# The start of a fused LoRA and expert kernel: fewer first loads, one tile's gather in two parts, another order

## The reference

```
g  = x Wg^T + 0.5 (x Ag[i]^T) Bg[i]^T          # i = itok_B_2_6[batch], rank 16
u  = x Wu^T + 0.5 (x Au[i]^T) Bu[i]^T
a  = silu(g) * u                               # 1376 columns
x += a Wd^T + 0.5 (a Ad[i]^T) Bd[i]^T          # layer 0
x += x W1[c]                                   # layer 1, c = itok_B_0_15[batch]
x += x W2^T + 2 * top-2 experts of 8 (LoRA)    # layer 2, bias by itok_B_0_7
x += x W3[c]                                   # layer 3
```

## Time and profile before

| what | value |
|---|---|
| median of three runs | 581.99 us (581.69 to 582.32) |
| the profiled execution | 581.79 us |
| its span | 579.5 us |
| PE busy | 569.5 us, 98% |
| DVE, ACT, POOL busy | 304.3, 206.5, 222.6 us |
| DMA | 77.38 MB, mean 134 GB/s |

### The profile page before, as it was taken

How to read it: one execution, slowest core, us unless ns; L and a number is a source line. 1 busy time by engine, 2 the same in 40 slices (tenths; PEclk the granted TensorE clock), 3 DMA queues, 4 the chain that set the end, 5 groups by cost and what they waited for, 6 DMA issues and landing times.

```text
span 579.5 us, 8822 instructions
## 1 busy us (share of the span) xinstructions
PE 569.5 (98%) x3381; PEld 513.9 (89%) x3381; DVE 304.3 (53%) x698; ACT 206.5 (36%) x413; POOL 222.6 (38%) x227
## 2 busy tenths in 40 slices
PE   7999999999999999999999999999999999999996
PEld 6888989898989898989898989898989899999995
DVE  5896353534343434444444444444444667777776
ACT  5774133333333333333232323233332533333331
POOL 4442153656565656441313131413130212443431
PEclk9999999999999999999999999999999999999999
DMA  8974343343534343442424242424242821243322
GB/s 268 379 248 143 110 144 95 122 153 123 154 122 154 122 153 128 147 155 77 138 77 137 77 139 76 137 78 137 77 138 73 300 84 54 74 136 139 111 90 74
DMA packets 35033, 77.38 MB, mean 134 GB/s; under 512 B 5360, under 2 KB 9776, under 8 KB 34992
## 3 DMA queue, kind: packets, MB, share of 16 engines
q0 software_dynamic: 10752, 37.23, 20.1%
q1 hardware_dynamic: 24096, 39.56, 20.1%
q10 hardware_dynamic: 144, 0.03, 0.0%
HBM read 64.22 MB, written 12.58 MB: 133 GB/s over the span
## 4 chain that ended last, share of the span: by engine, by line
PE 91%; DVE 3%; DMA 2%; issue 1%; SPq 1%; ACT 1%; POOLq 0%; POOL 0%; DVEq 0%; ACTq 0%
PE gu_ps L1161 13%; PE gu_ps L1163 13%; PE gu_ps L1162 13%; PE down_ps L1161 8%; PE down_ps L1162 8%; PE down_ps L1163 8%; PE l_ps L1161 5%; PE l_ps L1162 5%; PE l_ps L1163 5%; PE act_t L1233 3%; PE gu_ps L1168 3%; PE gu_ps L1169 3%; DMA b_sel_raw<-b_gu,idx_rank 1%; PE x2t_ps L1287 1%; DMA xt_raw<-x_t 1%
## 5 line engine op out<-in xcount | busy, mean ns | idle before, releaser
L679 POOL DMA_INDIRECT b_sel_raw<-b_gu,idx_rank x48 | 46.2, 962 | 188.1 <-PE gu_ps L1169 175.8
L1161 PE MATMUL down_ps<-wd_sb,act_hl 128*128 128x288 f32 (+1 forms) x352 | 105.1, 299 | 0.0
L1161 PE MATMUL gu_ps<-w_sb,xt 128*128 128x512 f32 x256 | 104.3, 408 | 0.0
L1162 PE MATMUL down_ps<-wd_sb,act_hl 128*128 128x288 f32 (+1 forms) x352 | 103.8, 295 | 0.0
L1163 PE MATMUL down_ps<-wd_sb,act_hl 128*128 128x288 f32 (+1 forms) x352 | 103.6, 294 | 0.0
L1163 PE MATMUL gu_ps<-w_sb,xt 128*128 128x512 f32 x256 | 100.6, 393 | 0.0
L1162 PE MATMUL gu_ps<-w_sb,xt 128*128 128x512 f32 x256 | 100.4, 392 | 0.0
L679 POOL DMA_INDIRECT a_raw<-a_all,idx_batch x64 | 76.6, 1196 | 58.9 <-DVE wd_sb L943 38.1
L795 ACT CAST act_hl<-act_t 128x256 fp32r<-128x256 f32 (+1 forms) x64 | 27.3, 453 | 133.3 <-PE act_t L1233 132.2
L786 ACT ACTIVATE act<-gu_ps 128x512 f32<-128x512 f32 (+1 forms) x47 | 26.1, 556 | 126.2 <-PE gu_ps L1169 126.2
L943 DVE TENSOR_TENSOR act_hl<-act_t,act_hl 128x256 fp32r<-128x256 f32 (+1 forms) x64 | 32.0, 521 | 71.1 <-ACT act_hl L795 71.0
(11 more groups left out here) (150 smaller groups left out, 1113.3 us busy)
## 6 DMA issues: line engine op xcount, KB each, us to landing
w_sb_raw<-wgu SPq DMA_DIRECT2D x16, 256.0 KB, 10.5
x_res<-x_rows SPq DMA_DIRECT2D x16, 256.0 KB, 2.8
x_after_l<-x_res SPq DMA_DIRECT2D x16, 256.0 KB, 2.3
bd<-bd_hl SPq DMA_DIRECT2D x16, 256.0 KB, 2.0
x<-x_after_l SPq DMA_DIRECT2D x16, 256.0 KB, 2.7
bd_hl<-bd SPq DMA_DIRECT2D x16, 256.0 KB, 4.7
xt_raw<-x_t SPq DMA_DIRECT2D x15, 256.0 KB, 2.5
out<-y SPq DMA_DIRECT2D x15, 256.0 KB, 2.0
```

The source lines that it names most:

```text
L679: nc.gpsimd.indirect_dma_start(out=dst, out_offset=None, in_=table, in_offset=bass.IndirectOffsetOnAxis(ap=idx, axis=0)).then_inc(s, 16)
L1161: pe.matmul(out_, stationary[0], moving[0], start=start, stop=False, skip_group_check=True)
L1162: pe.matmul(out_, stationary[0], moving[1], start=False, stop=False, skip_group_check=True)
```

## The change

- **Loads.** x of tile 0 is one transfer of 256 KB (its split stays in two halves). The up pieces of chunk 0 come in pairs, two transfers instead of four. x 1 comes before them, in SP's list and in the split list. All constants but the unit matrix, and the batch indices, already broadcast by the host, are one table `head` of 87 columns, which ACT's queue loads; the unit matrix is loaded by SP before the first up piece of chunk 1.
- **Indices.** `batch_indices` runs before the split of gate piece 0 of chunk 0, `rank_indices` before that of up piece 0.
- **Gathers.** For tiles 0 and 1 an A gather is two: 128 floats (64 KB) from a table of their own, and 176 floats (88 KB) from another. The order is gate-up A 0 (4), b 0, b 1, gate-up A 1 (4), down A 0 (4), b 2, down A 1 (2), b 3, down A 1 (2), bd 0, b 4. Later tiles are as before.
- **Splits**, steps 0 to 4, and **PE**, in another order.

```diff
 def first_items():
     w = wgu_items(0, 0)
-    return [("x", 0, 0), w[0], w[1], ("x", 0, 1), w[2], w[3]] + wgu_items(0, 1) + [("x", 1, 0)]
+    return [("x", 0, 0), w[0], w[1], ("x", 0, 1), w[2], w[3], ("x", 1, 0)] + wgu_items(0, 1)
...
-def a_items(i):
-    return [("a", i, b) for b in range(TB)]
+def a_items(i, part):
+    return [("a", i, b, part) for b in range(TB)]
...
-        return {-1: a_items(0) + [("b", 0), ("b", 1)] + a_items(1),
-                0: [("b", 2)],
-                1: [("b", 3)],
+        return {-1: a_items(0, 0) + [("b", 0), ("b", 1)] + a_items(1, 0) + a_items(0, 1),
+                0: [("b", 2)] + a_items(1, 1)[:2],
+                1: [("b", 3)] + a_items(1, 1)[2:],
                 2: [("bd", 0), ("b", 4)],
-                3: [("b", 5)] + a_items(2),
+                3: [("b", 5)] + a_items(2, None),
...
-                0: (wgu_items(1, 0) + [("at", 0)] + w1u[:2] + [("tm", 0), ("b", 0), ("t", 0)] + w1u[2:]
-                    + [("b", 1), ("gate", 0)]),
-                1: ([("at", 1)] + wgu_items(2, 0) + [("gate", 1), ("tm", 1), ("adt", 0)] + wgu_items(2, 1)
-                    + [("t", 1)]),
-                2: [("b", 2), ("b", 3), ("adt", 1), ("gate", 2), ("act", 0)] + wd_items(0),
+                0: (wgu_items(1, 0) + [("at", 0)] + w1u[:2] + [("b", 0), w1u[2], ("tm", 0), w1u[3], ("b", 1), ("t", 0),
+                    ("at", 1), w2g[0], ("gate", 0)]),
+                1: w2g[1:] + [("gate", 1), ("tm", 1)] + wgu_items(2, 1) + [("t", 1)],
+                2: [("b", 2), ("adt", 0), ("b", 3), ("adt", 1), ("gate", 2), ("act", 0)] + wd_items(0),
                 3: [("gate", 3)] + wd_items(1) + [("act", 1), ("b", 4)],
-                4: [("gate", 4), ("bd", 0)] + wd_items(2) + [("act", 2), ("b", 5), ("x", 2, 0)],
+                4: wd_items(2) + [("act", 2), ("gate", 4), ("bd", 0), ("b", 5), ("x", 2, 0)],
...
+                    if (n, m) == (0, 1):
+                        if c % 2:
+                            return
+                        dst = wu0_raw[:, 1, c:c + 2, :]
+                        src = wgu[:, at:at + 2 * width(n)].rearrange("p (c n) -> p c n", n=width(n))
...
-                    if it == ("wgu", 0, 0, 1):
-                        sp.dma_start(const_sb[:, 0:early], consts[:, 0:early]).then_inc(s_const, 16)
-                    if it == ("x", 1, 0):
-                        sp.dma_start(const_sb[:, early:], consts[:, early:]).then_inc(s_ident, 16)
+                    if it == ("wgu", 1, 1, 0):
+                        sp.dma_start(ident_sb[:], unit).then_inc(s_ident, 16)
...
+                    if i >= 2:
+                        gather(dst[:, b, :], a_all, idx_batch[:, at:at + 1], s_a_in)
+                    elif part == 0:
+                        gather(dst[:, b, 0:A_GU], a_gu, idx_batch[:, at:at + 1], s_a_gu_in[i])
+                    else:
+                        gather(dst[:, b, A_GU:], a_d, idx_batch[:, at:at + 1], s_a_d_in[i])
...
-            sc.dma_start(itok[:, 0, :], it_lora.partition_broadcast(P)).then_inc(s_const, 16)
+            sc.dma_start(head_sb[:], head).then_inc(s_const, 16)
...
-                    if job == ("wgu", 0, 0, 2):
+                    if job == ("wgu", 0, 0, 0):
+                        batch_indices()
+                    if job == ("wgu", 0, 1, 0):
                         rank_indices()
...
             whole(gate, 0)
+            whole(gate, 2)
             whole(up, 0)
-            whole(gate, 2)
             whole(up, 2)
-            gate(1, 0, HC // 2)
+            whole(gate, 1)
             x_a(0)
-            gate(1, HC // 2, HC)
+            up(1, 0, HC // 2)
             transpose_t(0)
-            up(1, 0, HC // 2)
+            up(1, HC // 2, HC)
             adapters(0)
-            up(1, HC // 2, HC)
             adapters(1)
             x_a(1)
...
             whole(up, 4)
-            adapters(4)
             down(1)
             transpose_act(2)
+            adapters(4)
             gate(5, 0, HC // 2)
             down(2)
```

More of the change, by code:

```diff
@@ L199, in gathers @@
     if n < 2 and i + 1 < NT:
-        out += [("a", i + 1, b) for b in range(n * TB // 2, (n + 1) * TB // 2)]
+        out += a_items(i + 1, None)[n * TB // 2:(n + 1) * TB // 2]
     if n == 2:
@@ L252, with bass_conditioned_residual_chain @@
 NO_SPLIT = ("gate", "tm", "tdm", "x1")
-def bass_conditioned_residual_chain(nc, x_t, x_rows, it_lora, it_cond, it_lang, wgu, wd, a_all, b_d,
-                                    w13, w2ra_t, b2, consts, *rest):
+def bass_conditioned_residual_chain(nc, x_t, x_rows, it_cond, it_lang, wgu, wd, a_all, a_gu, a_d, b_d,
+                                    w13, w2ra_t, b2, head, unit, *rest):
     b_gu, (out,) = rest[:NC], rest[NC:]
@@ L290, in const, with ids_of @@
             a, b = CONST_COLS[name]
-            return const_sb[:, a:b]
-        ident = const("ident")
+            return head_sb[:, a:b]
+        def ids_of(n):
+            return itok[:, n - 1, :] if n else head_sb[:, CONSTS.shape[1]:].bitcast(I32)
+        ident = ident_sb[:]
         mem_a = ExitStack()
@@ L395, in bass_conditioned_residual_chain @@
         s_wd_in = [sem(f"s_wd_in{f}") for f in range(FC)]
-        s_x0_in = [sem(f"s_x0_in{h}") for h in range(2)]
         s_xt_in = [sem(f"s_xt_in{i}") for i in range(2)]
         s_a_in = sem("s_a_in")
-        s_a1_in = sem("s_a1_in")
+        s_a_gu_in = [sem(f"s_a_gu_in{i}") for i in range(2)]
+        s_a_d_in = [sem(f"s_a_d_in{i}") for i in range(2)]
         s_b_in = [sem(f"s_b_in{i}") for i in range(2)]
@@ L528, in landing @@
             if kind == "wgu":
-                return s_wgu_in[it[1]][it[2]][it[3]], 16
+                c = it[3] - it[3] % 2 if it[1:3] == (0, 1) else it[3]
+                return s_wgu_in[it[1]][it[2]][c], 16
             if kind == "wd":
@@ L532, in landing @@
             if kind == "x":
-                return (s_x0_in[it[2]], 16) if it[1] == 0 else (s_xt_in[it[1] % 2], 16 * ((it[1] + 1) // 2))
+                return s_xt_in[it[1] % 2], 16 * (it[1] // 2 + 1)
             if kind == "b":
@@ L685, in gather_item @@
                 if kind == "a":
-                    _, i, b = it
-                    if b == 0 and i == 0:
+                    _, i, b, part = it
+                    if b == 0 and i == 0 and part == 0:
                         pool.wait_ge(s_idx, IDX_BATCH)
@@ L691, in gather_item @@
                     at = i * TB + b
-                    dst, landed = (a_raw1, s_a1_in) if i == 1 else (a_raw, s_a_in)
-                    gather(dst[:, b, :], a_all, idx_batch[:, at:at + 1], landed)
+                    dst = a_raw1 if i == 1 else a_raw
+                    if i >= 2:
[4 more added lines that the diff above has]
+                        gather(dst[:, b, A_GU:], a_d, idx_batch[:, at:at + 1], s_a_d_in[i])
                 elif kind == "b":
@@ L1097, in _ @@
             ve.memset(warm[:], 0.0).then_inc(s_warm, 1)
-            batch_indices()
             def low_w2(n):
@@ L1494 @@
         "b2": a["L2_cond_B"].transpose(0, 2, 1).reshape(EXPERTS * RANK, H),
-        "consts": CONSTS,
+        "head": np.concatenate([CONSTS, np.broadcast_to(a["itok_B_2_6"].astype(np.int32).view(np.float32),
+                                                        (P, BATCHES))], axis=1),
+        "unit": np.eye(P, dtype=np.float32),
     }
```

39 lines of the change are left out of this document (21 added, 18 removed).

## The result

The changed kernel takes **585.8 us** (median of 6 executions, 583.0 to 586.1), the kernel before 581.8 beside it: a ratio of 1.0056, 95% interval 1.0036 to 1.0077. It was to be 580.6. Measured again it was 585.3 (10 executions, 581.3 to 586.2), 1.0048 [1.0026, 1.0070]. Of these 16 executions none reached the 580.6 of the prediction; the fastest took 581.25. The change makes the kernel slower by half a per cent, and the time lies outside the range. The profiled execution took 585.95 us, with a span of 583.7.

What follows compares the result with a forecast made beforehand. TensorE was taken to bound the kernel (busy 569.5 of 579.5 us), so only its early idle time could pay. down(0) 0, adapters(4) -1.05 and down(2) -0.2 gave 580.6 us, range 579.4 to 582.4 (8 in 10).

Steps and rivals of the forecast that it cites:

- Part 1: First loads: first product 0.2 to 0.3 us later, gate(1) about 0.9 us sooner (bounds 0 to 1.5), lost before down(0).
- Part 2: Batch index behind the split of x's first half: first gather at 6.5 instead of 5.97, every gather 0.5 us later.
- Part 3: Eight more gathers on POOL: b 3 issued at 28.6, landing at 33.2 as before; down(0) change 0, bounds -0.7 to +2.4.
- the serial reading: Gathers taken one after another at about 2.0 us fixed each: eight more would cost 16 us of queue; rejected.
- Part 4: PE runs down(1) and act(2)'s transposes before adapters(4): gain 1.05 us at adapters(4) and 0.2 at down(2).
- The sum: down(0) 0, adapters(4) -1.05, down(2) -0.2: 580.5 us; with the median 0.2 above the profiled execution, stated as 580.6.
- Part 5: Unit matrix loaded later, early splits reordered: transpose_t(0) may wait 0.3 us, adapters(0) 0.5, paid from Part 1's 0.9.
- Rival 3: Tile 1's last A-down gather takes 6.1 us, down(0) starts 2.7 us later: 583.3 us, slower; chance 0.10.
- Rivals 1, 2 and 4: 1: both gathers land early, 580.0, 0.17; 2: wait moves to down(0), 581.5, 0.23; 4: b 4 late, 581.6, 0.03.

Runs made afterwards that it cites:

- run of 12: The kernel with whole rows plus two gathers that nobody reads, behind tile 1's on GpSimd: 581.4 us (579.7 to 583.2).
- the kernel with whole rows: The changed kernel with A of tiles 0 and 1 gathered whole again, eight gathers fewer, all else kept: 579.7 us, ratio 0.9956.
- the best one: The changed kernel with tile 1's A gathered whole and tile 0's four A-down gathers moved behind b 3: 579.4 us, ratio 0.9958.
- the late order alone: The kernel before with only down(1) and act(2)'s transposes moved ahead of adapters(4), and step 4's splits reordered: 580.8 us, ratio 0.9978.
- The changed kernel with the pause: The changed kernel with GpSimd waiting, ahead of the first A-down gather, for the transpose of tile 0's masked products: 583.9 us.
- 14 warm-up products: The changed kernel with 14 warm-up products instead of 10, so that PE starts later; POOL issues 21 gathers without a pause: 584.8 us.
- the burst at 211.71: The kernel with whole rows plus twelve 16-byte gathers (bytes per partition) that nobody reads at step 20, near 200 us: 593.6 us.
- the rows cut elsewhere: The changed kernel with A's rows cut so that early gathers bring 704 bytes and late ones 512: 585.0 us (581.2 to 586.8).
- 16-byte gathers: The kernel with whole rows plus four gathers of 16 bytes a partition that nobody reads: 584.8 us, in a second batch 585.3.

## Why the prediction was wrong, point by point

The medians that carry the account, in us: run of 10 gathers 579.7 and 579.4 (580.8 with the old loads), run of 12 581.4, run of 14 582.9 to 586.8.

- **Part 1 (loads): right in direction, too small at the start.** The first cast of x was at 3.66, not 5.15, and no later than its first half had been. How much sooner is not clear: it lies at 3.58 to 3.81 in the fourteen profiles with the new loads, and at 3.83, 4.11 and 4.80 in the three with the old ones; the kernel before had drawn a late one. The first product starts at 5.89 instead of 6.8 to 7.0, gate(1) at 14.37, a lead of 2.0 us instead of 0.9 (beyond the bound of 1.5); with the old loads gate(1) starts at 16.2 to 16.5, in the changed kernel, the one with whole rows and the best one at 14.2 to 14.4. Where no gap eats it, part of the lead reaches the end: the kernel with whole rows is 1.1 us faster than the late order alone, and the best one has down(2) at 49.02 against 50.05. I had given it nothing.
- **Part 2 (index): wrong sign.** It follows from the early x: index at 4.43, first gather at 4.97 instead of 6.5 (5.45 to 5.97 with the old loads).
- **Part 3 (A in two parts): the step that failed.** Its terms were not far off one by one. POOL issues the fourteen gathers at one per 1.34 us (1.3 was taken), so halving the bytes does not halve them. b 3 is cast 4.4 us after its issue (4.6 was taken), and from that cast to down(0) it is 5.2 us, as before. But the sum took b 2's gather to wait for POOL alone. It waits for adapters(0) too, and those came 6.8 us late (28.99 against 22.24): b 2 was issued at 30.64, b 3 at 34.47 instead of 28.6, down(0) started 5.7 us late instead of 0. What the step left out is that eight more gathers can hold up *other* engines: the mask of tile 0 at 25.40 instead of 19.5. No row of the kernel before shows this; its first run was of ten. The term was 0 with bounds of -0.7 and +2.4; it measured 5.7, through the late mask and not through b 3's latency. Even without the gap the 0 may have been too good: the executions of the changed kernel whose clock shows no stretch at one half took 581.25, 581.84 and 583.01. None of them has a trace.
- **The rule of the Trainium skill** (page "DMA: Bandwidth & Descriptors", section "Anatomy of one DMA") gives each such DMA about 2.0 us fixed. The prediction weighed this as queue time and dropped it. It was rightly dropped: no row here shows gathers of 2.0 us in series. That the added gathers lost time all the same has another reason, so the serial reading would have been right by luck.
- **Part 4 (order on PE): right.** 1.25 us were forecast, the late order alone gave 1.1 in time and 1.29 at down(2). In the changed kernel it is there as well: 5.66 us late at down(0), 4.32 at down(2), so 1.34 come back between.
- **The sum.** By its own terms it gives 580.7 and not 580.6 (581.79 less 1.25, plus 0.2). That changes nothing here. That what PE gains or loses by down(2) arrives at the end was right: 4.3 us at down(2), 4.2 in the span.
- **Part 5: not tested by itself.** transpose_t(0) in the kernel with whole rows had no wait of its own, and adapters(0) waited 1.07 us for the split of t instead of 0.5.
- **The rivals.** Rival 3 (slower, 583.3) had the sign and a late b 3, but by its own mechanism it did not happen: no wait for the last A-down gather stands in the chain. The changed kernel with the pause comes near its size, 583.9, in part through b 3's issue at 31.4. Rivals 1, 2 and 4 are out.

**What stays open** is why. Shown: the gap follows the number of gathers that POOL issues without a pause. Executions with a mean clock of 0.997 or less: none of 32 with a run of 10 (four kernels), 5 of 10 with 12, 41 of 53 with 14, 7 of 10 with 21. It needs neither large rows nor many bytes in the gathers that are added, nor PE's lead, nor bulk loads, and arithmetic on POOL does not make it. But a run of 10 is no guarantee: of the 89 executions of the kernel before in these batches, four have a clock of 0.996 or 0.997 (581.97, 582.07, 584.19 and 584.23 us). None of them was profiled.

On where the delay sits the traces say more than the changed kernel's first profile. Its PE goes at a pace of 1.4 us, and so, in small, does PE with a run of 12. In the other profiles with a gap PE starts the last product of x_a(0) in time (18.35 to 18.76; for tile 1 with 14 warm-up products at 26.36, for the burst at 211.71), and the mask follows 3.4 to 8.6 us later instead of 0.3 to 1.8. So what is late is mostly the signal of a product that has started in time. Why is not shown. Counting completion packets in the traces, at most five gathers were under way at once in the executions without a gap, and six at some point in those with one (the one at step 20 not counted; for under 0.03 us with the rows cut elsewhere and with 14 warm-up products, there 9 us ahead of the gap). Whether that number is a cause wasn't tried. Nor is it shown that the gap is there without the profiler's records: every execution of the experiments has a span and a clock from them.

## What to carry to other kernels

A gather from GpSimd's queue costs 1.25 us and more of that queue whatever it brings, so splitting one to have a part of it earlier doubles its price; split only the one that is waited for (tile 0 here), and put its second part behind a pause of the queue; here even that earned nothing clear (579.4 against 579.7). Count how many gathers stand in the queue without a pause: with twelve and more, expect TensorE's semaphores to come late, and look for "remote" and "issue" waits and for a fall of the granted clock in that stretch. When an engine waits for a result that has, by its neighbours' rows, long been there, change the traffic around it and not the work.

## What the runs showed of the hardware that I had not expected

- A run of 14 gathers on GpSimd, four of them of 2 KB, can delay TensorE's signal to VectorE, and with it TensorE's next work and ScalarE's, by 4 to 6 us (mask at 25.4 instead of 19.5 to 20), and does so in some executions and not in others of the same kernel: 579.9 to 581.3 and 584.7 to 585.1 us.
- In the gap TensorE may go on at one group of products per 1.4 us instead of one product per 0.11 us, with no wait that the profile knows.
- In and behind the gap the granted clock stood at one half (20.5 to 30.7 us in the changed kernel, 24.4 to 31.3 in the second profile with 16-byte gathers) and then came back; matmuls of 128x512 followed each other every 0.43 us instead of 0.23. It cost nothing beyond the gap: from the mask to down(0) it was 17.9 us, and 18.65 in the same kernel at full clock.
- x of tile 0 as one load of 256 KB, the first in the queue, was cast at 3.58 to 3.81 us; its first half as a load of 128 KB, first as well, at 3.83 to 4.80.
